# Gathering expert rows by a list of tokens instead of scattering them into slots, in a graph and mixture network

## The reference, cut to what matters

```python
# layer 0: x is 3327 x 256
h = gelu(einsum('td,edh->teh', flat_x, w1) + b1)        # 8 experts, hidden width 1024
expert_out = einsum('teh,ehd->ted', h, w2) + b2
combined = einsum('ted,te->td', expert_out, gate_output) # gate_output: the two best weights, else 0
# layer 1, after attention
for i in range(N_EXPERTS):
    mask = (topk_idx == i).any(-1)
    sel = sort(where(mask, tok, T))[:capacity]
    xi = xf[minimum(sel, T - 1)]
    yi = gelu(xi @ w1[i] + b1[i]) @ w2[i] + b2[i]
    out = out.at[sel].set(yi, mode='drop')
```

## Time and profile before

| | us |
|---|---|
| median of 3 runs | 2963.14 (2962.20 to 2964.66) |
| the profiled execution | 2960.15 |
| its span | 2958.5 |
| PE busy | 2472.5 (84%) |
| DVE busy | 1993.0 |
| ACT busy | 1573.0 |
| POOL busy | 1251.6 |

### The profile page before, as it was taken

How to read it: one execution, slowest core, us unless ns; L and a number is a source line. 1 busy time by engine, 2 the same in 40 slices (tenths; PEclk the granted TensorE clock), 3 DMA queues, 4 the chain that set the end, 5 groups by cost and what they waited for, 6 DMA issues and landing times. The chain is left out here.

```text
span 2958.5 us, 54884 instructions
## 1 busy us (share of the span) xinstructions
PE 2472.5 (84%) x20856; PEld 1919.4 (65%) x20856; DVE 1993.0 (67%) x2987; ACT 1573.0 (53%) x2652; POOL 1251.6 (42%) x738
## 2 busy tenths in 40 slices
PE   4789805999997998758999999999999997409992
PEld 3668704999995877644666666666666664409992
DVE  5775424888877865438777777777777773328883
ACT  4554304777764543323666666666666665206761
POOL 0001051000004402234888888888888886230003
PEclk9999957999998999876999999999999999559996
DMA  9988115666646753224000000220000000126663
GB/s 398 362 309 341 47 67 193 230 229 238 240 162 217 235 185 129 97 90 122 14 16 10 14 16 16 46 48 16 10 14 16 10 12 1 46 83 223 241 232 105
DMA packets 118767, 375.96 MB, mean 127 GB/s; under 512 B 22256, under 2 KB 56432, under 8 KB 100656
## 3 DMA queue, kind: packets, MB, share of 16 engines
q1 hardware_dynamic: 96192, 302.78, 28.9%
q0 software_dynamic: 20800, 65.82, 6.0%
q10 hardware_dynamic: 1584, 4.75, 0.4%
HBM read 314.30 MB, written 58.98 MB: 126 GB/s over the span
## 5 line engine op out<-in xcount | busy, mean ns | idle before, releaser
L1255 POOL TENSOR_TENSOR at_pool_sum<-at_pool_sum,at_probs 128x1024 f32<-128x1024 f32 x364 | 866.7, 2381 | 97.0 <-ACT at_probs L1381 55.7
L1410 DVE TENSOR_REDUCE at_part_max<-ps_x 128x2 f32<-128x1024 f32 x624 | 734.4, 1221 | 228.1 <-PE ps_x L1311 227.8
L1381 ACT ACTIVATE at_probs<-ps_s 128x512 f32<-128x512 f32 x1352 | 698.4, 603 | 323.3 <-PE ps_s L1270 292.8
L1270 PE MATMUL ps_s<-at_qst,at_kst 97*128 97x256 f32 x2704 | 517.6, 311 | 5.2 <-ACT at_probs L1381 4.0
L1270 PEld LDWEIGHTS ps_s<-at_qst,at_kst 97*128 97x128 f32 x2704 | 368.9, 189 | 218.5 <-ACT at_probs L1381 127.2
L1287 PE MATMUL ps_oz<-at_probs,k_xhat 128*32 128x256 f32 (+1 forms) x5408 | 391.4, 386 | 0.0
L570 PE MATMUL ps_acc<-adj_hi,y_hi 128*128 128x512 f32 (+1 forms) x728 | 290.1, 399 | 93.6 <-DMA k_bias<-bias 32.8
L636 DVE TENSOR_TENSOR adj_lo<-adj_raw,adj_hi 128x1024 fp32r<-128x1024 f32 (+1 forms) x182 | 208.7, 1148 | 184.1 <-ACT adj_hi L410 181.7
L1040 POOL DMA_DIRECT2D results<-ex_res x54 | 39.3, 727 | 645.4 <-DVE ex_res L1027 645.4
L571 PE MATMUL ps_acc<-adj_lo,y_hi 128*128 128x512 f32 (+1 forms) x728 | 278.1, 382 | 0.0
L572 PE MATMUL ps_acc<-adj_hi,y_lo 128*128 128x512 f32 (+1 forms) x728 | 277.9, 382 | 0.0
(11 more groups left out here) (201 smaller groups left out, 4047.6 us busy)
## 6 DMA issues: line engine op xcount, KB each, us to landing
ex_w<-w SPq DMA_DIRECT2D x108, 1024.0 KB, 6.8
adj_raw<-adjT SPq DMA_DIRECT2D x156, 512.0 KB, 4.9
k_xhat<-adj SPq DMA_DIRECT2D x26, 1664.0 KB, 8.6
slots<-zeros POOLq DMA_DIRECT2D x27, 512.0 KB, 24.2
ex_rows<-slots SPq DMA_DIRECT2D x54, 256.0 KB, 2.9
results<-ex_res POOLq DMA_DIRECT2D x54, 256.0 KB, 2.8
at_qst<-qk_parts SPq DMA_DIRECT2D x78, 128.0 KB, 2.5
ex_b<-b SPq DMA_DIRECT2D x54, 128.0 KB, 2.1
```

The lines of the kernel that those rows point to most:

```text
L1255: pool.tensor_tensor(pool_sum[:, g % 2], pool_sum[:, g % 2], probs[:, tile % RING], ALU.add).then_inc(pool_added, 1)
L1270: last = pe.matmul(ps_s[:, unit % S_BANKS, hh, :], kst[:, 2 * j + hh, k * P:(k + 1) * P], qst[:, g % 2, 2 * j + hh, :], start=True, stop=True)
L1381: act.activation(probs[:, tile % RING, 2 * j:2 * j + 2], ps_s[:, unit % S_BANKS], ACT.Exp, scale=scale).then_inc(taken, 1)
L1410: dve.tensor_reduce(part_max[:, g % 2, heads, qt, kc], ps_x[:, pair, :], AX.X, ALU.max).then_inc(x_free, 1)
```

## The change

The slots in DRAM, their clearing and the scatter go. The normalised rows are written to DRAM once, in the order of the tokens (`moe_rows`): in the first graph layer by POOL, chunk by chunk, in the second mixture by SP beside the router's products. At the head of `expert_layers` a list from slot to token is made. DVE splits each slot number into a column (slot / 128) and a lane (slot mod 128), and marks both in bf16 arrays (`col_hot`, `lane_hot`, and `planes`, the column marks times the tile number), in groups of 13 entries, 4 groups in the first mixture and 2 in the second; ACT makes the other plane, the column marks times the token's number in its tile. PE multiplies lane marks by planes, 52 or 26 matmuls of 128x128 by 128x136 (128x80 in the second) into one PSUM tile, and DVE turns the sums into token numbers (`index`). POOL then gathers the rows of each chunk by two indirect DMAs, two chunks ahead, between its stores. The marks lie in the second weight buffer, `hid` and `m.xhat`, so SP loads the second chunk's weights only after the list is made; `turn` waits for the rows alone. An unused slot has index 0.

In the graph layers ACT does `taken_at` and `copied_at` ahead of its other epilogue work of a position. In the second layer `keep` moves from POOL to SP, at position 11 of the epilogue, with two semaphores; the first normalisation and all behind it move back by 3 positions. In the first layer PE waits for the parameters only before its first product with W.

```diff
+        @block.sync
+        def _(sp):
+            sp.dma_start(rows.rearrange("(k p) d -> p k d", p=P), src[:]).then_inc(rows_kept, 16)
+            sp.wait_ge(rows_kept, 16)
...
-    applies = at_positions([(at + 10 + q, p) for at, c, p, q in pairs])
-    roots2_begin, roots2_end = at_positions([(turns[c] + 12, c) for c in range(CHUNKS)]), at_positions([(turns[c] + 13, c) for c in range(CHUNKS)])
-    applies2 = at_positions([(at + 14 + q, p) for at, c, p, q in pairs])
+    applies = at_positions([(at + (10 if first else 13) + q, p) for at, c, p, q in pairs])
+    keeps = at_positions([(turns[c] + 11, c) for c in range(CHUNKS)])
+    roots2_begin, roots2_end = at_positions([(turns[c] + 15, c) for c in range(CHUNKS)]), at_positions([(turns[c] + 16, c) for c in range(CHUNKS)])
+    applies2 = at_positions([(at + 17 + q, p) for at, c, p, q in pairs])
+    norms = sorted((turns[c] + (15 if second else 8), second, c) for c in range(CHUNKS) for second in range(1 if first else 2))
+    norm = {(c, second): n for n, (_, second, c) in enumerate(norms)}
...
-        turned_at = at_positions([(at + 12 + 3 * q, p) for at, c, p, q in pairs])
-        copied_at = at_positions([(at + 16 + 3 * q, p) for at, c, p, q in pairs])
-        produced_at = at_positions([(at + 13 + 3 * q + i, 2 * p + i) for at, c, p, q in pairs for i in range(2)])
-        taken_at = at_positions([(at + 17 + 3 * q + i, 2 * p + i) for at, c, p, q in pairs for i in range(2)])
-        split_at = at_positions([(at + 18 + 3 * q + i, 2 * p + i) for at, c, p, q in pairs for i in range(2)])
+        turned_at = at_positions([(at + 15 + 3 * q, p) for at, c, p, q in pairs])
+        copied_at = at_positions([(at + 19 + 3 * q, p) for at, c, p, q in pairs])
+        produced_at = at_positions([(at + 16 + 3 * q + i, 2 * p + i) for at, c, p, q in pairs for i in range(2)])
+        taken_at = at_positions([(at + 20 + 3 * q + i, 2 * p + i) for at, c, p, q in pairs for i in range(2)])
+        split_at = at_positions([(at + 21 + 3 * q + i, 2 * p + i) for at, c, p, q in pairs for i in range(2)])
...
-                pool.memset(zeros[:], 0.0).then_inc(zero_made, 1)
...
-                pool.wait_ge(used, PIECES * TOGETHER)
...
-                        width = min(ZERO_COLS, cols - n)
-                        pool.dma_start(view[:, n:n + width], zeros[:, 0:width]).then_inc(cleared, 16)
...
-                pool.wait_ge(cleared, done)
+                for c in range(CHUNKS):
+                    at = slice(first_tile(c), first_tile(c + 1))
+                    pool.wait_ge(normed, at.stop)
+                    pool.dma_start(m.rows_d[at.start * P:at.stop * P, :].rearrange("(k p) d -> p k d", p=P), m.xhat[:, at, :]).then_inc(rows_kept, 16)
+                pool.wait_ge(rows_kept, 16 * CHUNKS)
...
-            def keep(c):
-                at = slice(first_tile(c), first_tile(c + 1))
-                pool.wait_ge(chain, first_tile(c + 1))
-                pool.dma_start(m.x_kept[:, at.start * D:at.stop * D], m.x[:, at, :].rearrange("p t d -> p (t d)")).then_inc(x_kept, 16)
...
-            keep(0)
...
                 add_output_bias(c)
-                if c + 1 < CHUNKS:
-                    keep(c + 1)
...
+            def keep(c):
+                at = slice(first_tile(c), first_tile(c + 1))
+                sp.wait_ge(chain, at.stop)
+                sp.dma_start(m.x_kept[:, at.start * D:at.stop * D], m.x[:, at, :].rearrange("p t d -> p (t d)")).then_inc(x_kept[c % 2], 16)
+
...
+                if not first:
+                    for c in keeps(g):
+                        keep(c)
...
+                for n in taken_at(g):
+                    take_logits(n) if first else round_product(n)
+                for p in copied_at(g):
+                    copy_turned(p)
                 for c in evacuations(g):
                     evacuate(c)
...
-                        act.wait_ge(x_kept, 16 * c + 16)
-                        apply(p, m.x, m.x, normed, 2 * c + 1)
+                        act.wait_ge(x_kept[c % 2], c // 2 * 16 + 16)
+                        apply(p, m.x, m.x, normed, norm[c, 0] + 1)
...
-                for n in taken_at(g):
-                    take_logits(n) if first else round_product(n)
-                for p in copied_at(g):
-                    copy_turned(p)
...
+                elif first:
+                    pe.wait_ge(params_loaded, 16 * 7)
...
-            if first:
-                pe.wait_ge(params_loaded, 16 * 7)
...
-        @block.gpsimd
-        def _(pool):
-            for put in puts:
-                for k in range(NT):
-                    pool.indirect_dma_start(out=slots, out_offset=bass.IndirectOffsetOnAxis(put[:, k:k + 1], 0),
-                                            in_=rows[:, k, :], in_offset=None).then_inc(sent, 16)
-            pool.wait_ge(sent, 16 * NT * len(puts))
...
+        lane_hot = w[:, 1].rearrange("p a n -> p (a n)").bitcast(BF16)[:, 0:MARKS * P].rearrange("p (i n) -> p i n", n=P)
+        planes = m.xhat[:].rearrange("p k n -> p (k n)").bitcast(BF16)[:, 0:MARKS * 2 * COLS].rearrange("p (i a n) -> p i a n", a=2, n=COLS)
+        col_hot = hid[:].rearrange("p h n -> p (h n)").bitcast(BF16)[:, 0:MARKS * COLS].rearrange("p (i n) -> p i n", n=COLS)
...
                     sp.wait_ge(weights_lo, n * 2 + 2)
                     e = sp.value_load(m.owner[0:1, ds(n, 1)], min_val=0, max_val=EXPERTS - 1)
-                    sp.dma_start(rows[:, k], slots[ds(i * 2 * CHUNK + k * CHUNK, CHUNK), :].rearrange("(a p) d -> p a d", p=P)).then_inc(loaded[k], 16)
                     for dst, src in ((w[:, k, 0, :], w1_d), (w[:, k, 1, :], w2_d)):
                         sp.dma_start(dst, src[ds(e, 1)].rearrange("a p n -> (a p) n")).then_inc(loaded[k], 16)
...
+            def find_rows():
+                for i in range(MARKS):
+                    if i % GROUP == 0:
+                        pe.wait_ge(planes_made, i // GROUP + 1)
+                        pe.wait_ge(lanes_made, i // GROUP + 1)
+                    last = pe.matmul(ps_o[:, 0, 0:2 * COLS], lane_hot[:, i, :], planes[:, i].rearrange("p a n -> p (a n)"),
+                                     start=i == 0, stop=i == MARKS - 1)
+                last.then_inc(found, 1)
...
-                arrived(pe, n, k)
+                pe.wait_ge(rows_come[k], n * 16 + (32 - 16 * k))
...
+            find_rows()
             turn(0, 0)
...
+            def lanes():
+                for g in range(MARKS // GROUP):
+                    act.wait_ge(matched, g + 1)
+                    at = slice(g * GROUP, (g + 1) * GROUP)
+                    act.activation(planes[:, at, 0, :], col_hot[:, at, :], ACT.Copy, scale=m.token_f[:, 0:1]).then_inc(lanes_made, 1)
+
+            lanes()
             prepare(0, 0)
...
-            dve.sem_inc(weights_lo, 4)
+            dve.sem_inc(weights_lo, 2)
...
+            def mark_rows():
+                c = Count(coded)
+                put = m.put[:, 0:n_rows, :].rearrange("p a k -> p (a k)")
+                c.inc(dve.tensor_scalar(code_i[:, 0], put, 7, None, ALU.arith_shift_right))
+                c.inc(dve.tensor_scalar(code_i[:, 1], put, P - 1, None, ALU.bitwise_and))
...
+                c.inc(dve.tensor_copy(code[:], code_i[:]))
...
+                for g in range(MARKS // GROUP):
+                    at = slice(g * GROUP, (g + 1) * GROUP)
...
+                    dve.tensor_tensor(col_hot[:, at, :], along(code[:, 0, at], COLS), numbers(COLS), ALU.is_equal).then_inc(matched, 1)
+                    dve.tensor_tensor(lane_hot[:, at, :], along(code[:, 1, at], P), numbers(P), ALU.is_equal)
+                    dve.wait_ge(matched, g + 1)
+                    tile = g * GROUP % NT
+                    dve.tensor_tensor(planes[:, at, 1, :], col_hot[:, at, :], along(m.iota_b[:, tile:tile + GROUP], COLS), ALU.mult).then_inc(planes_made, 1)
...
+            def list_rows():
+                dve.wait_ge(found, 1)
+                dve.tensor_copy(slot_of[:].rearrange("p a n -> p (a n)"), ps_o[:, 0, 0:2 * COLS]).then_inc(coded, 1)
+                dve.wait_ge(coded, 4)
+                dve.scalar_tensor_tensor(index[:], slot_of[:, 1], float(P), slot_of[:, 0], ALU.mult, ALU.add).then_inc(listed, 1)
...
+            mark_rows()
+            list_rows()
+            dve.sem_inc(weights_lo, 2)
             prepare(0, 0)
...
+            def fetch(n):
+                if n >= 2:
+                    pool.wait_ge(turned, n - 1)
+                for a in range(TT):
+                    pool.indirect_dma_start(out=rows[:, n % 2, a, :], out_offset=None, in_=m.rows_d,
+                                            in_offset=bass.IndirectOffsetOnAxis(index[:, TT * n + a:TT * n + a + 1], 0)).then_inc(rows_come[n % 2], 16)
...
+            def store(n):
+                k = n % 2
+                pool.wait_ge(out_made, n + 3)
+                pool.dma_start(results[n * CHUNK:(n + 1) * CHUNK, :].rearrange("(a p) d -> p a d", p=P), res[:, k]).then_inc(stored[k], 16)
```

(27 more changed lines are left out.)

100 lines of the change are left out of this document (48 added, 52 removed).

## The result

The changed kernel takes 2854.05 us (median of 4 runs, 2853.04 to 2859.31), the kernel before 2963.64 (4 runs beside it). The ratio is 0.9634, with 95% between 0.9617 and 0.9651. That is 109.6 us less, where 134 were forecast: the direction and most of the size are right, and the time lies just above the upper end of the range, 2854.

What follows compares the result with a forecast made beforehand. It took POOL's work and transfers to bound the heads, PE the experts, and waits for x's write the second layer. -59.3 - 33.8 - 39.0 - 1.5 = -133.6 from 2963.14 gave 2829 us, range 2813 to 2854.

Steps and rivals of the forecast that it cites:

- The heads: Before each mixture's experts: 29.2 us against 88.5 in the first (-59.3), 20.1 against 53.9 in the second (-33.8).
- the entry with its three small operations: Start of each mixture's head: block entry 0.4 us and three small operations of 0.2 each, 1.0 us together.
- the rival of a dearer list: Heads: marks and matmuls cost half as much again (2842) or twice as much (2855); chance of twice 0.08.
- marks at twice the rate: Heads: VectorE's bf16 marks run at double the float rate, 10.7 us less, so 2819; chance 0.07.
- two gathers, 4.4: Heads, from list to rows: POOL takes 1.25 us and a gather lands 3.1 us after its start.
- The starving gathers: Experts' stretch: VectorE's casts lengthen POOL's gathers, so PE waits; 3018 us at 6.3 us a gather; chance 0.02.
- five waits of PE go: 33.5, and 10.1 of lower clock: Second graph layer: PE's five waits for copies behind x's write go, with the slower clock after them; 43.6 us gained.
- signs of being wrong: PE waiting for `ex_rows`, lower clock with short waits in the second layer, a tail over 60 us after its last job.
- new waits in the second layer: Second graph layer: PE waits for lifts and roundings in narrow jobs, half of 43.6 us is lost, 2851; chance 0.12.
- -6.1 + 10.1: Second layer, move by 3 positions: 6.1 us leave the part with jobs, a tail period of 10.1 is added.
- First layer: First graph layer: copies ahead of square roots, last write of rows and PE's earlier start give -1.5 us together.

Runs made afterwards that it cites:

- rows_first: The changed kernel, but SP issues the second chunk's weights only when the first chunk's rows have landed, in both mixtures; 2847.25 us.
- add_later: The changed kernel with POOL's additions of the output bias moved from the second graph layer to the start of attention; 2841.85 us.
- shift_undone: The changed kernel with the second layer's epilogue at its old positions, 3 earlier, and nothing else changed; 2835.77 us.

## Why the prediction was right and wrong

- **The heads.** Right in mechanism and nearly in size. Marks, matmuls, list and the way from turn to matmul are within 0.3 us of their terms, the entry with its three small operations took 1.5 where 1.0 was set, and by them the rival of a dearer list and that of marks at twice the rate are both wrong. The term that failed is "two gathers, 4.4": 8.1 and 9.1 us. The landing time was read from gathers that had the DMA engines for themselves; I wrote myself that the second chunk's weights are asked for only after the list, and took from it that they are in time, not that they meet the first gather. +3.7 and +4.7; rows_first took both back.
- **Experts' stretch, gathers.** Right: 402.0 against 401.8. The starving gathers did not come. The rival had POOL's gathers held by VectorE's casts, and beside them they are longer, but by up to 0.27 us where it needed more than 3; the rows land in 5.8 us at the median, beside weights, and the two chunks of lead hide that.
- **Second layer.** The step that failed is "five waits of PE go: 33.5, and 10.1 of lower clock". By the lists of PE's waits on the timeline, the jobs lose 37.4 us of waits and get 16.4 back, of which 11.2 are the three for `qk_lo`: -21.0, and the clock gives 5.4 of the 10.1, since at three places of five the projections are still slow (4.7 us together). From first to last matmul of the jobs it was 358.1 us and is 326.4: -31.7 against -49.7. The tail went from 49.3 to 61.3, +12.0 against +10.7. Two of the prediction's own signs of being wrong came: lower clock with short waits in the layer, and a tail of over 60 us. The rival "new waits in the second layer" was the right one, and its term of 17 us for the layer is near the 19.6 measured, but it gave half of the reason. Narrow cover alone leaves waits of 3.0 us for `qk_lo` (add_later); the rest needs VectorE held by POOL. That its 2851 is only 3 us off the whole time is partly luck, since it has neither the gathers nor the end. The trace of before has a sign of the holding, the tiny operation of 2.28 us shown above, which I didn't price since the additions stayed where they were. I had not asked what they would stand beside once VectorE no longer stands still.
- **The move by 3 positions** I took as given with the part, and priced at some 4 us net (-6.1 + 10.1). It cost 18.3 us in this kernel (shift_undone), about half of it in the tail, and was not needed.
- **First layer.** -3.7 in this profile. Over the profiles, three with the old code show 369.2 to 370.8 and thirteen with the new 365.5 to 369.0 (mean 367.1): some -2.7, inside -4 to +1.5.
- **The end**, +2.8, had no term: it is POOL's DRAIN at the end of the expert block, 4.96 us in place of 1.69.

By place, measured less forecast: 18.2 in the second layer with its entry, 8.1 in the heads, 2.8 at the end, less 2.2 won in the first layer and 0.5 in the experts, make the 26.4 us between forecast and profile.

## What to carry to other kernels

When a wait is taken away, look at what its idle time was hiding: work of another engine that fell into it now meets something. A duration read from a quiet moment holds for the new place only if that is quiet too, so ask what else is issued within the same few microseconds and let the short transfer that is waited for go first. And try the smallest form of a move: here the other queue alone did what the queue with three later positions was meant to do, and was faster.

## What the chip showed that was not expected

- Operations of VectorE with both inputs in SBUF take 1.4 to 3.1 us longer beside a POOL addition of 2.40 us, whichever of the two began first by the records, and no longer beside a POOL fill of 0.97 us; with an input in PSUM they are not held.
- Two indirect gathers of 128 rows of 1 KB each are there 4.4 us after the list when no weights are under way, and 8.1 to 9.1 us when 2 MB of weights are issued 0.4 us after the first of them.
- POOL's DRAIN at the end of a block differs between programs: 4.96 against 1.69 us behind the second expert block, 1.53 against 2.83 behind the first, the same in every profile of a kind.
- A POOL gather that began 0.05 to 0.17 us after a VectorE cast of 0.43 us took 1.09 to 1.22 us in place of 0.95 and ended 1.26 to 1.27 us after the cast's start.
